# Transposing loads of a mixture-of-experts loop's rows, three sums buffers and six blocks per turn

## The chip, the cores and the metric

One core of a Trainium2 chip runs the whole kernel. The time is device microseconds (us) of one execution; the lower the better.

## The reference

Two samples of 1024 tokens with 256 channels pass a block with adaptive layer norm: linear attention with 8 heads of 32, then a mixture of 32 experts. All is float32. Cut to the part that the change touches:

```python
x = x + ga * attention(layernorm(x) * (1 + ca) + sa)
h = layernorm(x) * (1 + cb) + sb                 # (2048, 256)
scores = sigmoid(h @ w_router)                   # (2048, 32)
# per token: 4 of 8 groups by their two best, then the 6 best experts in them
combine[t, e] = scores[t, e] for the 6 chosen, else 0
g = einsum('th,ehm->etm', h, gate_w)             # m = 176
u = einsum('th,ehm->etm', h, up_w)
eo = einsum('etm,emh->eth', silu(g) * u, down_w)
routed = einsum('te,eth->th', combine, eo)
shared = silu(h @ sh_gate_w) * (h @ sh_up_w) @ sh_down_w
out = x + gb * (routed + shared)
```

## The kernel before

All five engines run programs written out by hand; semaphores order them, and PSUM banks are assigned by a plan (lines 215 to 320). Attention and the router work on tiles of 128 tokens in groups of four (GT); a sample b has two groups g. The names and lines that matter here:

- *Rows.* XH (line 85) holds per token 256 channels (X), 32 scores, and a record. `second_norm` on VectorE (L934) writes the normalised tokens h into X itself; TensorE turns them (`turn_h2`, L1311), ScalarE copies them out (`turned`, L686) and makes the scores (`scores`, L694; its activation is L698). `attend` (L871) holds, at its fourth tile, a reciprocal (L886) that waits for the store of the gate rows to DRAM (SP, L425).
- *Dispatch.* GpSimd writes each token's row to DRAM (`pair_rows`) six times, one indirect DMA per tile and choice, ordered by expert (L558).
- *The shared expert* (`hidden`, `shared_rows`) writes its rows to `token_sums[0]` (L711); the gated residual, divided by the gate, goes to `token_sums[1]` from SP (L431).
- *The loop over blocks.* A block is 128 (token, expert) pairs of one expert. A map in SBUF gives each block's expert and first row; the number of turns is known at run time only. `blocks` (L373) writes a step of R = 4 blocks five times on each engine: first, looped, twice under If, last. SP loads a block's rows (`load_rows`, L448) into one of four places once TensorE has turned what was there, and its records (`load_records`, L451). TensorE turns rows (`turn_x`, L1432) and, for blocks two apart, works through: turn the rows of n+2, turn the activations of n (`turn_act`, L1448), down of n-1 (`down_rows`, L1455), gate and up of n+2 (`gate_and_up`, L1440). VectorE copies the turned rows from PSUM (`copy_x`, L1105), multiplies (L1111), picks weights and token numbers (L1117, L1123). ScalarE does silu (L755), copies the turned activations (L762) and weighs the result (L769). GpSimd adds it into one of two sums in DRAM with an accumulating indirect DMA (`scatter`, L584); even blocks take `token_sums[0]`, odd ones `token_sums[1]`, and a scatter waits for the landing of the one two before it, which wrote the same sums. Blocks beyond the last non-empty one in a turn are run too, with destinations out of bounds.
- *The last stage.* SP fetches both sums in 8 groups of two tiles (L476; two groups of the first sums ahead of the last scatters), VectorE adds and multiplies by the gate (L1155, L1156), SP stores (L494).

## Time and profile before

| | |
|---|---|
| median of 3 runs | 584.3 us (577.68, 584.3, 585.07) |
| the profiled execution | 584.41 us, span 582.6 us |
| TensorE (PE) busy | 472.4 us, 81% |
| GpSimd (POOL) busy | 284.2 us, 49% |
| VectorE (DVE) busy | 232.7 us, 40% |
| ScalarE (ACT) busy | 176.3 us, 30% |
| matmuls of gate and up, L1444 | 416, 142.7 us busy |
| transposes of the rows, L1437 | 208, 40.7 us busy |
| DMA | 83.25 MB, mean 143 GB/s |

Times are from the start of the span. PEld is TensorE's weight load, SPq SyncE's DMA issue. Busy times of matmuls overlap, since matmuls are pipelined; the distance of their starts is what they cost. A float32 matmul appears twice, a transpose once. The idle time of an engine stands in brackets with what released it. The granted clock is TensorE's, as a share of full speed.

### The profile page before, as it was taken

The page shows a single profiled execution, that of the slowest core. Times are in us where ns is not written, and L with a number is a line of the kernel's source. Part 1 is how long each engine was busy: PE and PEld are TensorE (multiplying, and loading weights), DVE is VectorE, ACT ScalarE, POOL GpSimd, SP SyncE. Part 2 cuts the span into 40 slices and gives each one's busy share as a digit, 9 for nine tenths or more (in the row PEclk, how much of TensorE's full clock was granted, in tenths as well). Part 3 has the DMA queues.
Part 4 walks back from the last instruction along what each step waited for, and adds up shares of the span by engine and source line. Part 5 has one row for each costly group of instructions (what it writes and reads, how often), then busy time and mean ns, then how long its engine had stood idle before and what let it go on. Part 6 is the DMA issues. An engine that isn't in the chain of part 4 may idle for free.

```text
span 582.6 us, 9494 instructions
## 1 busy us (share of the span) xinstructions
PE 472.4 (81%) x1994; PEld 325.4 (56%) x1995; DVE 232.7 (40%) x983; ACT 176.3 (30%) x429; POOL 284.2 (49%) x253
## 2 busy tenths in 40 slices
PE   4898989827785459829699999999999999999800
PEld 3455755417534216415477777777777777777600
DVE  2726789405871027301133334334333333333206
ACT  2231322201220003001144444444444444444300
POOL 2303512770777731760045655665666666655630
PEclk9799978967895759958899999999999999999865
DMA  8999010330458842841257766567665757677459
GB/s 282 342 333 380 31 73 24 124 124 11 152 143 270 282 162 83 292 168 61 67 89 108 111 96 109 101 108 105 113 105 103 109 94 114 105 117 110 52 131 334
DMA packets 87922, 83.25 MB, mean 143 GB/s; under 512 B 22522, under 2 KB 80348, under 8 KB 87901
## 3 DMA queue, kind: packets, MB, share of 16 engines
q1 hardware_dynamic: 66012, 52.59, 31.1%
q0 software_dynamic: 19584, 28.33, 26.2%
q10 hardware_dynamic: 2304, 2.10, 1.1%
q8 instruction: 8, 0.13, 0.1%
q14 instruction: 14, 0.11, 0.1%
HBM read 43.13 MB, written 40.90 MB: 144 GB/s over the span
## 4 chain that ended last, share of the span: by engine, by line
PE 72%; issue 10%; DVE 7%; another core or an unknown queue 4%; DMA 4%; ACT 2%; SPq 1%; POOL 0%; POOLq 0%; ACTq 0%; DVEq 0%
PE bank L1444 21%; PE bank L1459 16%; PE bank L1361 8%; PE bank L1372 5%; PE bank L1437 4%; PE bank L1452 4%; PE bank L1261 4%; PE bank L1247 2%; PE bank L1334 2%; PE bank L1163 2%; DMA token_sums<-tok_buf,dest 1%; DMA XH<-in_L_attn_x 1%; PE bank L1280 1%; PE bank L1195 1%
## 5 line engine op out<-in xcount | busy, mean ns | idle before, releaser
L592 POOL DMA_INDIRECT token_sums<-tok_buf,dest x104 | 161.9, 1557 | 138.2 <-ACT tok_buf L775 52.2
L1444 PE MATMUL bank<-gate_up,tok_buf 128*128 x416 | 142.7, 466 | 0.4 <-DVE tok_buf L1109 0.4
L564 POOL DMA_INDIRECT pair_rows<-XH,rows_i x96 | 94.6, 985 | 62.7 <-DVE rows_i L1028 34.3
L1109 DVE COPY tok_buf<-bank 128x256 f32<-128x256 f32 x104 | 44.2, 425 | 172.2 <-PE bank L1437 143.8
L1459 PE MATMUL bank<-down,tok_buf 88*128 x416 | 109.9, 387 | 0.0
L1444 PEld LDWEIGHTS bank<-gate_up,tok_buf 128*128 128x128 f32 x416 | 80.0, 193 | 29.4 <-issue 2.1
L1459 PEld LDWEIGHTS bank<-down,tok_buf 88*128 88x128 f32 x416 | 71.0, 191 | 7.7 <-issue 0.2
L775 ACT ACTIVATE tok_buf<-bank,tok_buf 128x256 f32<-128x256 f32 x104 | 49.2, 473 | 55.0 <-PE bank L1459 28.7
L1361 PE MATMUL bank<-tok_buf,sh_gu 128*128 128x512 f32 (+1 forms) x96 | 50.1, 673 | 10.8 <-issue 10.8
L760 ACT ACTIVATE tok_buf<-bank 128x176 f32<-128x176 f32 x104 | 33.0, 317 | 79.9 <-PE bank L1444 73.3
L1437 PEld LDWEIGHTS bank<-ident,tok_buf 128*128 128x128 f32 x208 | 27.3, 141 | 37.9 <-issue 29.7
L1437 PE MATMUL bank<-ident,tok_buf 128*128 128x128 f32 x208 | 40.7, 277 | 6.6 <-issue 5.9
L766 ACT ACTIVATE tok_buf<-bank 88x256 f32<-88x256 f32 x104 | 39.4, 379 | 18.0 <-PE bank L1452 8.1
L1372 PE MATMUL bank<-sh_dn,sT 128*128 128x256 f32 (+1 forms) x96 | 27.9, 447 | 17.5 <-issue 17.5
L1361 PEld LDWEIGHTS bank<-tok_buf,sh_gu 128*128 128x128 f32 (+1 forms) x96 | 19.9, 209 | 39.6 <-issue 39.4
L1452 PE MATMUL bank<-ident,tok_buf 128*88 128x128 f32 x208 | 39.7, 273 | 0.0
L1115 DVE TENSOR_TENSOR tok_buf<-tok_buf,bank 128x176 f32<-128x176 f32 x104 | 34.1, 327 | 3.5 <-ACT tok_buf L760 3.5
L1372 PEld LDWEIGHTS bank<-sh_dn,sT 128*128 128x128 f32 (+1 forms) x96 | 21.1, 225 | 22.9 <-issue 19.2
L1261 PE MATMUL bank<-down 128*128 128x512 f32 x64 | 33.0, 652 | 0.0
L515 POOL TENSOR_SCALAR rstd<-gate_up 128x4 f32<-128x4 f32 x8 | 4.6, 571 | 43.9 <-DVE gate_up L932 30.3
L1119 DVE SCALAR_TENSOR_TENSOR tok_buf<-iota_e,own_expert,tok_buf 128x32 f32<-128x32 f32 x104 | 25.7, 247 | 0.4
L551 POOL TENSOR_TENSOR XH<-XH,down 128x256 f32<-128x256 f32 x16 | 11.0, 719 | 29.3 <-DVE down L869 29.3
(153 smaller groups left out, 462.6 us busy)
## 6 DMA issues: line engine op xcount, KB each, us to landing
tok_buf<-pair_rows SPq DMA_DIRECT2D x104, 128.0 KB
gate_up<-in_L_ffn_gate_w SPq DMA_DIRECT2D x8, 704.0 KB, 8.5
gate_up<-in_L_ffn_up_w SPq DMA_DIRECT2D x8, 704.0 KB, 9.1
down<-in_L_ffn_down_w SPq DMA_DIRECT2D x2, 2816.0 KB
pair_rows<-sh_rows SPq DMA_DIRECT2D x1, 5120.0 KB, 18.9
gate_up<-token_sums SPq DMA_DIRECT2D x16, 256.0 KB, 6.0
XH<-in_L_attn_x SPq DMA_DIRECT2D x4, 512.0 KB, 9.7
token_sums<-sh_rows ACTq DMA_DIRECT2D x16, 128.0 KB
```

The source lines that it names most:

```text
L564: nc.gpsimd.indirect_dma_start(out=pair_rows, out_offset=bass.IndirectOffsetOnAxis(ap=rows_i[:, t, k:k + 1], axis=0), in_=XH[:, t, :], in_ ...
L592: nc.gpsimd.indirect_dma_start(out=token_sums[c % 2], out_offset=bass.IndirectOffsetOnAxis(ap=dest[:, c:c + 1], axis=0), in_=yw[:, c, :], ...
L766: nc.scalar.activation(aT[0:KD, c % 2, :, :], banks[3][0:KD, 0:2 * P].rearrange("p (m n) -> p m n", m=2), ACT.Copy).then_inc(aT_copied, 1)
L775: nc.scalar.activation(yw[:, c, :], banks[4 + c % 2][:, 0:C], ACT.Copy, scale=pair_weight[:, c:c + 1]).then_inc(y_scaled, 1)
L1109: V.tensor_copy(xT[:, c % 2], banks[0][:, 0:C].rearrange("p (k n) -> p k n", k=KC)).then_inc(xT_copied, 1)
L1261: last = mm(ps[:, :], hT[:, k, a:a + P], wT[:, k, C:3 * C], start=k == 0, stop=k == KC - 1)
L1361: last = mm(ps[0:n, :], sh_gu[:, s, k, a:a + n], h2T[:, b, k, g * W:(g + 1) * W], start=k == 0, stop=k == KC - 1)
L1372: last = mm(ps[:, 0:C], sT[0:n, m, i * P:(i + 1) * P], sh_dn[0:n, m, :], start=m == 0, stop=m == len(SC) - 1)
L1437: last = nc.tensor.transpose(banks[0][:, k * P:(k + 1) * P], xg[:, s, k * P:(k + 1) * P], ident[:, :])
L1444: last = mm(banks[1 + c % 2][:, 0:M2], xT[:, c % 2, k, :], gate_up[:, bass.ds(e * (KC * M2) + k * M2, M2)], start=k == 0, stop=k == KC - 1)
L1452: last = nc.tensor.transpose(banks[3][0:KD, m * P:(m + 1) * P], act[:, c % 2, m * KD:(m + 1) * KD], ident[:, :])
L1459: last = mm(banks[4 + c % 2][:, 0:C], aT[0:KD, c % 2, m, :], down[0:KD, bass.ds(e * C + m * E * C, C)], start=m == 0, stop=m == 1)
```

## The change

- Rows go to DRAM as two planes of 16-bit halves: `second_norm` writes h to a buffer of its own (`h2`, one group), from which TensorE turns it, and ScalarE (`split`) writes the low halves of a token's 256 floats and then the high halves into X. VectorE waits with the next group's h for the split and the turned tiles of the last; GpSimd's dispatch waits for the split.
- In the loop SP loads a block's rows with a transposing DMA of 16-bit elements (128 rows x 512), and VectorE (`join_x`) interleaves low and high halves into float32. TensorE's `turn_x` and its PSUM bank are gone.
- R is 6: six places for rows, records, results; six blocks in a step; at least 17 turns where there were at least 24. The rings lie in XH's space.
- Three sums in place of two. A block adds into sums n mod 3, a scatter waits for the one three before it. `token_sums[2]` is filled with zeros by a DMA of SP behind that which clears the heads of `pair_rows`, ahead of the store of the gate rows.
- The last stage has 4 groups of four tiles. Each sums buffer is fetched whole once its last scatters have landed, the gate rows ahead of the third; VectorE adds the first two for all groups, then adds the third and multiplies.

The diff without its context lines (`@@ -n @@` is the line of the kernel before at which a part stands):

```diff
@@ -13 @@
-    f32, i32, u32, bf16 = mybir.dt.float32, mybir.dt.int32, mybir.dt.uint32, mybir.dt.bfloat16
+    f32, i32, u32, bf16, u16 = mybir.dt.float32, mybir.dt.int32, mybir.dt.uint32, mybir.dt.bfloat16, mybir.dt.uint16
@@ -37 @@
-    TURNS = -(-NBLK // 4)
-    FEWEST = T * TOPK // P // 4 - 1
-    MAP_W = P + 8
+    R = 6
+    NSUM = 3
+    TURNS = -(-NBLK // R)
+    FEWEST = T * TOPK // P // R - 1
+    MAP_W = P + 2 * R
@@ -73 @@
-        token_sums = [nc.dram_tensor(f"token_sums{a}", (T, C), f32).ap() for a in range(2)]
+        token_sums = [nc.dram_tensor(f"token_sums{a}", (T, C), f32).ap() for a in range(NSUM)]
@@ -94 @@
-        own_expert = sb("own_expert", [P, P])[:, :]
-        dest = sb("dest", [P, 4], i32)
+        own_experts = sb("own_expert", [P, P + R])
+        own_expert = own_experts[:, 0:P]
+        dest = sb("dest", [P, R], i32)
@@ -146 @@
+        h2 = part(GT * C).rearrange("p (i c) -> p i c", i=GT)
@@ -158 @@
-        part = shared_part(tok_buf, NT * C // 2)
-        R = 4
-        xg = part(R * C).rearrange("p (s c) -> p s c", s=R)
+        part = shared_part(XH[:, :, :].rearrange("p i w -> p (i w)"), NT * XW)
+        x_halves = part(R * C).bitcast(u16).rearrange("p (s q n) -> p s q n", s=R, q=2 * KC)
-        part = shared_part(tok_buf[:, NT * C // 2:], NT * C // 2)
@@ -175 @@
-        sums = gate_up[:, 0:2 * NT * C].rearrange("p (a i c) -> p a i c", a=2, i=NT)
+        sums = [*(gate_up[:, a * NT * C:(a + 1) * NT * C].rearrange("p (i c) -> p i c", i=NT) for a in range(2)), xn]
@@ -192 @@
-        var2_ready, rstd2_ready, h2_ready = (sem(n) for n in ("var2_ready", "rstd2_ready", "h2_ready"))
+        var2_ready, rstd2_ready, h2_ready, split_ready = (
+            sem(n) for n in ("var2_ready", "rstd2_ready", "h2_ready", "halves_ready"))
-        zeros_ready, heads_clear = sem("zeros_ready"), sem("segment_heads_clear")
+        zeros_ready, heads_clear, sums_clear = sem("zeros_ready"), sem("segment_heads_clear"), sem("last_sums_clear")
@@ -205 @@
-        x_turned, xT_copied, gu_done, silu_done, act_done, act_turned, aT_copied, y_done, y_scaled = (
-            sem(n) for n in ("x_turned", "xT_copied", "gate_up_done", "silu_done", "act_done", "act_turned", "aT_copied", "y_done", "y_scaled"))
-        OT = 2
-        fetched = [sem(f"sums_fetched{g}") for g in range(NT // OT)]
+        xT_joined, gu_done, silu_done, act_done, act_turned, aT_copied, y_done, y_scaled = (
+            sem(n) for n in ("xT_joined", "gate_up_done", "silu_done", "act_done", "act_turned", "aT_copied", "y_done", "y_scaled"))
+        OT = 4
+        fetched, last_fetched = ([sem(f"{n}_sums_fetched{g}") for g in range(NT // OT)] for n in ("first", "last"))
@@ -421 @@
+            sp.dma_start(token_sums[2].rearrange("(p n) c -> p n c", p=P),
+                         zeros[:, 0:C].unsqueeze(1).broadcast_to([P, NT, C])).then_inc(sums_clear, 16)
@@ -446 @@
-                sp.dma_start(xg[:, c, :], pair_rows[bass.DynSlice(col, P, E), 0:C]).then_inc(x_loaded[c], 16)
+                sp.dma_start_transpose(x_halves[:, c], pair_rows[bass.DynSlice(col, P, E), 0:C].bitcast(u16)).then_inc(x_loaded[c], 16)
@@ -462 @@
-                        sp.wait_ge(x_turned, n + 1)
+                        sp.wait_ge(xT_joined, n + 1)
@@ -475 @@
-                sp.dma_start(sums[:, a, t:t + OT, :], sums_v[a][:, t // TB, t % TB:t % TB + OT, :]).then_inc(fetched[g], 16)
-            early = 2
-            for a in range(2):
-                for s in range(a, R, 2):
+                sp.dma_start(sums[a][:, t:t + OT, :], sums_v[a][:, t // TB, t % TB:t % TB + OT, :]).then_inc(
+                    (fetched if a < NSUM - 1 else last_fetched)[g], 16)
+            for a in range(NSUM):
+                for s in range(a, R, NSUM):
-                for g in range(early):
-                    fetch_sums(a, g)
-                if a == 0:
+                if a == NSUM - 1:
-            for g in range(early, NT // OT):
-                for a in range(2):
+                for g in range(NT // OT):
-                sp.dma_start(out_v[:, t // TB, t % TB:t % TB + OT, :], sums[:, 0, t:t + OT, :]).then_inc(stored, 16)
+                sp.dma_start(out_v[:, t // TB, t % TB:t % TB + OT, :], sums[0][:, t:t + OT, :]).then_inc(stored, 16)
@@ -561 @@
+                    pool.wait_ge(split_ready, (t // GT + 1) * GT)
-                        out=pair_rows, out_offset=bass.IndirectOffsetOnAxis(ap=rows_i[:, t, k:k + 1], axis=0),
-                        in_=XH[:, t, :], in_offset=None).then_inc(dispatched, 16)
+                        out=pair_rows.bitcast(i32), out_offset=bass.IndirectOffsetOnAxis(ap=rows_i[:, t, k:k + 1], axis=0),
+                        in_=XH[:, t, :].bitcast(i32), in_offset=None).then_inc(dispatched, 16)
@@ -576 @@
+            pool.wait_ge(sums_clear, 16)
@@ -587 @@
-                wait(pool, scattered[(c - 2) % R], 16 * turns)
+                wait(pool, scattered[(c - NSUM) % R], 16 * turns)
-                    out=token_sums[c % 2], out_offset=bass.IndirectOffsetOnAxis(ap=dest[:, c:c + 1], axis=0),
+                    out=token_sums[c % NSUM], out_offset=bass.IndirectOffsetOnAxis(ap=dest[:, c:c + 1], axis=0),
@@ -599 @@
-                        scatter((c - 1) % R, n - 1, turn + (c == R - 1))
+                        scatter((c - 1) % R, n - 1, turn + (c > NSUM))
@@ -698 @@
+            def split(b, g):
+                for i in range(GT):
+                    t = b * TB + g * GT + i
+                    act_e.wait_ge(h2_ready, t + 1)
+                    nc.scalar.activation(X[:, t, :].bitcast(u16).rearrange("p (h c) -> p h c", h=2),
+                                         h2[:, i, :].bitcast(u16).rearrange("p (c h) -> p h c", h=2),
+                                         ACT.Copy).then_inc(split_ready, 1)
@@ -716 @@
+                        act_e.wait_ge(sums_clear, 16)
@@ -729 @@
+            split(0, 0)
+            split(0, 1)
@@ -740 @@
+            split(1, 0)
+            split(1, 1)
@@ -771 @@
-                    act_e.wait_ge(pool_passed, n - 1)
+                    act_e.wait_ge(pool_passed, n - R + NSUM + 1)
@@ -940 @@
+                if b or g:
+                    dve.wait_ge(split_ready, b * TB + g * GT)
+                    for k in range(KC):
+                        await_computed(dve, ("h2T", b, 0, k) if g else ("h2T", b - 1, NG - 1, k))
-                    V.scalar_tensor_tensor(out=X[:, t, :], in0=X[:, t, :], scalar=rstd2[:, t:t + 1],
+                    V.scalar_tensor_tensor(out=h2[:, i % GT, :], in0=X[:, t, :], scalar=rstd2[:, t:t + 1],
@@ -1099 @@
+            link(V.memset(own_experts[:, P:P + R], -float(2 * T)))
-            def copy_x(c, n):
-                dve.wait_ge(x_turned, n + 1)
+            def join_x(s, c, n, turn):
+                dve.wait_ge(x_loaded[s], 16 * (turn + 1))
-                V.tensor_copy(xT[:, c % 2], banks[0][:, 0:C].rearrange("p (k n) -> p k n", k=KC)).then_inc(xT_copied, 1)
+                V.tensor_copy(xT[:, c % 2].bitcast(u16).rearrange("p k (n h) -> p h k n", h=2),
+                              x_halves[:, s].rearrange("p (h k) n -> p h k n", h=2)).then_inc(xT_joined, 1)
@@ -1116 @@
-                V.scalar_tensor_tensor(out=rec[:, c, 0:E], in0=iota_e[:, :], scalar=own_expert[:, bass.ds(n, 1)], in1=rec[:, c, 0:E],
+                V.scalar_tensor_tensor(out=rec[:, c, 0:E], in0=iota_e[:, :], scalar=own_experts[:, bass.ds(n, 1)], in1=rec[:, c, 0:E],
-                    dve.wait_ge(pool_passed, n - 1)
-                V.scalar_tensor_tensor(out=dest[:, c:c + 1], in0=own_expert[:, bass.ds(n, 1)], scalar=-1.0,
+                    dve.wait_ge(pool_passed, n - R + NSUM + 1)
+                V.scalar_tensor_tensor(out=dest[:, c:c + 1], in0=own_experts[:, bass.ds(n, 1)], scalar=-1.0,
-                copy_x(c, c)
+                join_x(c, c, c, 0)
@@ -1135 @@
-                        copy_x(c, n + 2)
+                        join_x((c + 2) % R, c, n + 2, turn + (c + 2) // R)
@@ -1147 @@
+            def group(a, g):
+                return sums[a][:, g * OT:(g + 1) * OT, :]
+            for g in range(NT // OT):
+                dve.wait_ge(fetched[g], 32)
+                last = V.tensor_tensor(group(0, g), group(0, g), group(1, g), ALU.add)
+            link(last)
-                rows_g = slice(g * OT, (g + 1) * OT)
-                total = sums[:, 0, rows_g, :]
-                dve.wait_ge(fetched[g], 32)
-                link(V.tensor_tensor(total, total, sums[:, 1, rows_g, :], ALU.add))
-                V.tensor_tensor(total, total, over(gb_again[:, g * OT // TB, :], [P, OT, C], 1), ALU.mult).then_inc(out_ready, 1)
+                dve.wait_ge(last_fetched[g], 16)
+                link(V.tensor_tensor(group(0, g), group(0, g), group(2, g), ALU.add))
+                V.tensor_tensor(group(0, g), group(0, g), over(gb_again[:, g * OT // TB, :], [P, OT, C], 1),
+                                ALU.mult).then_inc(out_ready, 1)
@@ -1316 @@
-                        last = turn(of(keys[k])[:, i * P:(i + 1) * P], X[:, b * TB + g * GT + i, k * P:(k + 1) * P])
+                        last = turn(of(keys[k])[:, i * P:(i + 1) * P], h2[:, i, k * P:(k + 1) * P])
@@ -1429 @@
-            def turn_x(s, n, turn):
-                pe.wait_ge(x_loaded[s], 16 * (turn + 1))
-                wait(pe, xT_copied, n)
-                for k in range(KC):
-                    last = nc.tensor.transpose(banks[0][:, k * P:(k + 1) * P], xg[:, s, k * P:(k + 1) * P], ident[:, :])
-                last.then_inc(x_turned, 1)
-                pe.wait_ge(xT_copied, n + 1)
+                pe.wait_ge(xT_joined, n + 1)
@@ -1463 @@
-                turn_x(c, c, 0)
-            for c in range(2):
@@ -1473 @@
-                    if not last or c + 2 < R:
-                        turn_x((c + 2) % R, n + 2, turn + (c + 2) // R)
```

## Rows read from the trace of the kernel before

**Rows 1.** Table by stretch: busy PE, PEld, DVE, ACT, POOL; clock, DMA share, GB/s.
```profile
180.00:216.00 36.00, 18.96 (x48) 11.85 (x48) 0.68 (x4) 1.41 (x3) 23.22 (x25) 0.59 0.74 244
...
300.00:350.00 50.00, 50.00 (x239) 37.18 (x237) 17.95 (x99) 23.01 (x59) 28.76 (x19) 1.00 0.68 105
...
500.00:540.00 40.00, 39.97 (x190) 29.89 (x189) 14.70 (x80) 18.40 (x47) 23.73 (x16) 1.00 0.69 111
```

**Rows 2.** Timeline of one block: start us, us, engine, line, operation, [idle before].
```profile
382.85 0.38 PE L1437 MATMUL bank<-ident,tok_buf 128*128 128x128 f32 x2
...
383.07 0.38 PE L1452 MATMUL bank<-ident,tok_buf 128*88 128x128 f32 x2
...
383.29 1.03 PE L1459 MATMUL bank<-down,tok_buf 88*128 x4
...
383.40 0.33 SPq L449 DMA_DIRECT2D tok_buf<-pair_rows  x1
...
384.15 1.35 PE L1444 MATMUL bank<-gate_up,tok_buf 128*128 x4
...
385.34 0.38 PE L1437 MATMUL bank<-ident,tok_buf 128*128 128x128 f32 x2
```

**Rows 3.** Chain of waits, the loop: start us, us, what.
```profile
330.80 1.19 PE bank L1444 x4
...
513.69 1.19 PE bank L1444 x4
```

**Rows 4.** Groups by line and shape, 300 to 540: busy, mean ns, idle before.
```profile
L592 POOL DMA_INDIRECT token_sums<-tok_buf,dest x94 | 146.3, 1556 | 96.3 <-DMA token_sums<-tok_buf,dest 41.8 <-DVE dest L1126 22.2 <-issue 16.5
...
L1109 DVE COPY tok_buf<-bank 128x256 f32<-128x256 f32 x94 | 39.9, 425 | 146.6 <-PE bank L1437 118.2 <-issue 22.2 <-PE bank L1444 6.2
```

**Rows 5.** Timeline of the end.
```profile
552.66 1.98 PE L1459 MATMUL bank<-down,tok_buf 88*128 x8
...
556.34 1.56 POOL L592 DMA_INDIRECT token_sums<-tok_buf,dest  x1 [0.80 <-DMA token_sums<-tok_buf,dest]
...
558.49 1.55 POOL L592 DMA_INDIRECT token_sums<-tok_buf,dest  x1 [0.59 <-issue]
...
563.19 7.38 SPq L478 DMA_DIRECT2D gate_up<-token_sums  x14
...
577.62 0.69 DVE L1156 TENSOR_TENSOR gate_up<-gate_up 128x512 f32<-128x512 f32 x1
```

**Rows 6.** Chain of waits, the end.
```profile
551.71 3.80 DMA token_sums<-tok_buf,dest
...
558.49 4.64 DMA token_sums<-tok_buf,dest
```

**Rows 7.** Table by stretch, the end.
```profile
558.00:560.00 2.00, 0.00 (x0) 0.00 (x0) 0.00 (x0) 0.00 (x0) 1.51 (x1) 0.70 0.04 1
...
568.00:570.00 2.00, 0.00 (x0) 0.00 (x0) 1.96 (x4) 0.00 (x0) 0.00 (x0) 0.50 1.04 352
```

**Rows 8.** DMA queues, 300 to 540: packets, MB, share of 16 engines.
```profile
q0 software_dynamic: 13414, 11.49, 41.1%
...
q1 hardware_dynamic: 27072, 13.92, 25.1%
```

**Rows 9.** Table by stretch, the first stage.
```profile
52.00:56.00 4.00, 2.17 (x14) 1.56 (x13) 2.65 (x12) 0.66 (x2) 2.75 (x5) 1.00 1.05 382
...
56.00:60.00 4.00, 3.49 (x19) 3.30 (x19) 2.29 (x9) 0.77 (x2) 4.00 (x7) 0.63 0.88 317
```

**Rows 10.** Timeline of VectorE and ScalarE ahead of the loop.
```profile
63.37 3.32 DVE L886 RECIPROCAL down<-down 128x512 f32<-128x512 f32 x1
...
87.17 0.38 ACT L654 ACTIVATE down<-bank 128x256 f32<-128x256 f32 x1 [3.30 <-PE bank L1261]
...
160.92 0.60 ACT L709 ACTIVATE sT<-bank 128x512 f32<-128x512 f32 x1 [2.00 <-PE bank L1361]
...
216.41 0.38 ACT L720 ACTIVATE sh_rows<-bank 128x256 f32<-128x256 f32 x1 [1.19 <-remote]
```

## The prediction

> **What bounds the kernel now.** Three views decide, in this order. The table by stretch [rows 1] shows TensorE busy all of the 50 us from 300 to 350, at a granted clock of 1.00 (the level of 2.4 GHz), and 39.97 of the 40 us from 500 to 540: the loop over blocks of pairs, almost half of the span, runs at TensorE's pace. Beside it GpSimd has 28.76 us of the same 50, ScalarE 23.01, VectorE 17.95, and the 16 DMA engines a share of 0.68. From 180 to 216 it is neither: TensorE has 18.96 of 36 us at a granted clock of 0.59.
>
> The timeline of one block [rows 2] gives the order on TensorE; matmuls are pipelined, so starts count, not ends. Two transposes of the rows start at 382.85, those of the activations at 383.07, down at 383.29, gate and up at 384.15, the next rows at 385.34. So the rows' transposes take 0.22 us, the activations' 0.22, down 0.86, gate and up 1.19: 2.49 us a block. The chain of waits holds it over a distance: gate and up of one place in the turn start at 330.80 and at 513.69 [rows 3], 18 turns apart, 10.16 us a turn. That is 0.20 above 4 x 2.49: the boundary of a turn.
>
> **The change, part by part.** I sum against the profiled execution, 584.41 us with a span of 582.6; it is within 0.2 us of the median of the three runs, 584.3.
>
> *Rows that arrive turned.* TensorE loses 0.22 us a block and nothing else on it changes, so a block takes 2.27 us if no other engine is late. VectorE's copy of 256 floats from PSUM, 425 ns [rows 4], becomes a copy of 512 halves with a step of two. The trace has no such copy; the bounds are 0.425, if a half counts half, and 0.69, what 512 elements with two operands take [rows 5]. I take 0.65, near the upper one since the number of elements is the same. VectorE's busy time was 17.95 of 50 us, 0.91 a block; it becomes 1.14, at most 1.18, of 2.27: covered. The new copy waits for a load and for a product two blocks back, where the old one stood between a transpose and the product of its own block. ScalarE has 23.01 of 50, 1.17 a block. GpSimd's scatter is 1.556 us [rows 4]; with the 0.59 idle before the last one [rows 5] it is 2.15, covered as well, though narrowly.
>
> *Number of blocks.* Routing the reference's own inputs gives 102 non-empty blocks (each expert's tokens over 128, rounded up). Four per turn make 104 of them, six make exactly 102. The trace agrees that the last are empty: after the very last scatter starts, at 558.49 [rows 5], the DMA moves 1 GB/s until 560 [rows 7], against 105 in the loop. Two blocks go, 5.0 us. Boundaries fall from 25 to 16, but each loads half as many values again; 25 x 0.20 - 16 x 0.25 = 1.0.
>
> Loop: 102 x 0.22 = 22.4, and 5.0, and 1.0, and 0.4 for two row transposes ahead of the first block: **-28.8 us**. If something else holds the old pace, the blocks alone remain, -5.
>
> *The transposing load.* No row shows one. From below, it costs the DMA engines what the plain load does: from 300 to 540 queue q1 (rows and records) had 25.1% of 240 us, 60.2 us for 94 blocks, 0.64 a block, and q0 (scatters) 41.1%, 1.05 a block [rows 8]; together 1.69 of 2.27. From above: each 1 KB row is four pieces of 128 16-bit elements, and a piece costs what a mean packet costs now, 60.2 x 16 / 27072 = 35.6 ns; 512 + 128 packets then take 1.42 us, with the scatter 2.47. Further still, the whole 0.64 four times is 2.56, with the scatter 3.6. I take about 1.0, nearer to the plain load, since a piece has a quarter of the bytes: 2.05 of 2.27, just covered. SP's issue is 0.33 us now [rows 2] with another for the records; there is room for 1.6 more a block. The latency is covered by the six places: one is filled again 6 x 2.27 = 13.6 us before its rows are wanted. Behind a load on SP that waits for its join stand only record loads, which VectorE wants some blocks later.
>
> The Trainium skill stands on both sides here. "DMA: Bandwidth & Descriptors", section "Latency and other measured facts", has 261 GB/s for transposing DMAs over non-contiguous parts: an estimate from that page is 0.50 us for a block's 128 KB, and the loop would keep the sum above. "VectorE: DVE Perf Modes", section "The three transpose paths", has 1309 ns for one 128x128 16-bit transpose through the crossbar; four in a row would be 5.2 us a block by that page, twice the old pace. No row here shows either.
>
> *Three sums.* A scatter now waits for the one three before it. With two, waits for a landing were 41.8 us of GpSimd's idle time [rows 4]. Two blocks at the new pace are 4.54 us, and a landing came 3.80 and 4.64 us after its start [rows 6], so two sums would nearly bind; three give 6.8. No gain by itself: it is cover for the 22.4.
>
> *First stage.* A 2.1 MB zero fill goes on SP's queue ahead of the store of the gate rows. The DMA engines are full until about 59.5 us (382 GB/s, then a share of 0.88 from 56 to 60) [rows 9]; 2.1 MB at 382 is 5.5 us, so they are full until 65. What is late is VectorE's reciprocal at 63.37 [rows 10], which waits for that store, and all of attend behind it. 65 and a landing less 63.4: **+2.5**; 0 if the store overtakes, 5.5 at most.
>
> *The split on ScalarE.* 16 copies of 512 halves; a 128x512 activation is 0.60 us [rows 10], so 2.4 a group. Three groups find ScalarE idle behind the scores anyway: 3.30 us before 87.17, 2.71 likewise in the second group, 2.00 before 160.92 [rows 10], where the 0.4 left over delays nobody, as no bank is waited for. In the fourth it was idle for 1.19 before the shared rows at 216.41, for which TensorE waits: **+1.2**, between 0 and 2.4. The other new waits (split_ready on VectorE and GpSimd, the turned tiles) are for work that ended microseconds before.
>
> *The end.* TensorE's last matmuls run from 552.66 to 554.64, the last scatter starts at 558.49, and SP goes on at 563.19 [rows 5], 8.5 us after TensorE. With three sums the wait before 556.34 goes: 7. From there to 582.6 were 19.4 us. Now 6 MB are fetched where 4 were. Two sums, 4.2 MB, begin some 4.3 us before the last landing T; at 352 GB/s [rows 7] they take 12, until T + 8; gate rows and the first quarter of the third sum land at T + 11. VectorE then adds and multiplies four groups of 1024 elements, eight operations of 1.2 to 1.3 us (twice 0.69, less a start): T + 21. The last store, 512 KB, takes the 4.3 us that 256 KB took from the last product's end, 578.3, or a little more: T + 26. So -1.5 + 6.5 = **+5**; +1 if VectorE's work hides in the fetches, +9 if fetches and stores get in each other's way.
>
> Sum: -28.8 + 2.5 + 1.2 + 5 = -20.1; 584.4 - 20.1 = **564 us**.
>
> **The rivals.**
> *A. The DMA engines fill.* With 1.42 us for the loads a block takes 2.47 us: 102 x 0.20 = 20.4 given back, 585. For it: a share of 0.68 already. Against: a quarter of a row is not a whole packet's work. Chance 0.14.
> *B. Slower.* The queue turns rows one piece after the other at four times the present cost, and records behind them are held up too: 3.6 us a block, 102 x 1.33 = 136 more, 700. It decides from 2.27 + 20.1/102 = 2.47 us a block on. Nothing in the trace speaks against it but the plain loads' 0.64. The page with 1309 ns is on this side. Chance 0.14.
> *C. The blocks are not 102.* With 103 by the kernel's own routing there are 18 turns and 108 blocks, 6 x 2.27 = 13.6 more: 578. One token at a threshold would do it. Chance 0.04.
> *D. Longer stalls ahead of the loop.* From 180 to 216 ScalarE was busy for 1.41 us and TensorE half idle with the DMA engines at 0.74 [rows 1], and no wait for data accounts for it. More code on ScalarE and more DMA may lengthen that by a third, 12 us: 576. Chance 0.06.
>
> **How the numbers follow.** The forecast has 0.62, with a range of its own of 554 to 573: 0, 0 and +1 at one end (-27.8, and 2 for what the bounds miss), 5.5, 2.4 and 9 at the other (-11.9). A measurement of this kernel tells about 2%, 11.7 us: faster means below 572.6. Faster 0.62, the forecast. Slower 0.17: B and what of A lies beyond 596. Same 0.21: the rest. Range 552 to 590; it leaves out B and little else.
>
> **What would show it.** Right: gate and up 2.27 us apart at a clock of 1.00, a turn of 13.7 to 13.9; TensorE full; a DMA share of 0.85 to 0.95; VectorE's copy near 0.65; 102 scatters; 26 us from the last landing to the end; the reciprocal 2 to 3 us later. Wrong: TensorE idle in the loop and the copy waiting for the rows' DMA; issues on SP above 1.9 us; a DMA share of 1; 108 scatters; a copy above 1 us.

## The result, and the profile after

The changed kernel takes 596.3 us (median of 4 runs, 590.26 to 598.12) against 584.7 for the kernel before: ratio 1.023, 95% interval 1.018 to 1.029. It is slower by 2.3%; the forecast was 564. Its profiled execution has a span of 594.2 us, 11.6 more than before.

Three milestones split these 11.6 us, each read in the timeline of TensorE (the forecast had +2.5 + 1.2 - 0.4 ahead of the loop):

| | before | after | forecast |
|---|---|---|---|
| first gate and up product of the loop | 285.1 | 299.7: +14.6 | +3.3 |
| from there to the end of the last down product | 269.5 | 259.8: -9.7 | -28.4 |
| from there to the end | 28.0 | 34.7: +6.7 | +5 |

So of the 31.7 us between forecast and result, 18.7 lie in the loop, 11.3 ahead of it and 1.7 behind it.

**The loop.** The table by stretch (same columns as [rows 1]) shows TensorE no longer full, where it had 50.00 and 39.97:

```profile
300.00:350.00 50.00, 47.46 (x197) 33.41 (x197) 21.46 (x96) 20.48 (x58) 26.92 (x17) 0.96 0.71 95
500.00:540.00 40.00, 37.42 (x157) 27.09 (x158) 16.19 (x75) 16.86 (x47) 22.75 (x15) 0.96 0.78 107
```

The timeline of two neighbouring blocks answers [rows 2]. The rows' transposes are gone, and gate and up start 2.27 us apart:

```profile
372.83 1.35 PE L1465 MATMUL bank<-gate_up,XH 128*128 x4
...
375.10 1.35 PE L1465 MATMUL bank<-gate_up,XH 128*128 x4
```

So a block costs what was forecast. But over the 43 steps from 350.9 to 457.9 us the mean is 2.49, not 2.27: seven of them take 3.1 to 4.1 us. The chain of waits (start us, us, what) names who is late. In the loop of before it ran along TensorE [rows 3]; now the turn below lies wholly on SP's instruction queue, and over the whole execution 34% of the chain does (1% before):

```profile
404.75 2.67 SPq L369
...
413.72 1.19 SPq L453
...
415.16 0.37 SPq L456
...
415.74 1.19 SPq L453
...
417.13 0.42 SPq L456
...
417.76 1.19 SPq L453
...
419.98 2.73 SPq L369
```

A row load and a record load are issued every 2.02 to 2.04 us (415.74 to 417.76), and at each turn SP reads 12 values of the map from SBUF into registers (line 369) for 2.7 us. From 404.75 to 419.98 are 15.23 us for six blocks, 2.54 each: slower than TensorE's 2.27. In 330 to 500 us the trace has no wait of SP at all. The rows for single source lines (engine, operation, count, shortest/median/longest ns, first and last start) give the two prices. Of the kernel before:

```profile
L367 SPq TENSOR_LOAD <-down x27: 1666/1871/2041, 261.5 to 538.6; - x27
L367 PEldq TENSOR_LOAD <-down x27: 587/594/2335, 281.4 to 543.7; - x27
```

Of the changed kernel:

```profile
L453 SPq DMA_TRANSPOSE XH<-pair_rows x102: 668/1190/2215, 276.0 to 541.9; - x102
L369 SPq TENSOR_LOAD <-down x18: 2471/2660/3030, 273.2 to 546.1; - x18
L369 PEldq TENSOR_LOAD <-down x18: 846/2086/3405, 296.2 to 545.8; - x18
```

The issue of a transposing load holds SP's queue for a median of 1.19 us, where a plain one holds it for 0.33 [rows 2]. And on TensorE's own queue (PEldq) the read went from a median of 0.59 us to anything between 0.85 and 3.4. The median hides what it does; the same row for four consecutive turns:

```profile
L369 PEldq TENSOR_LOAD <-down x1: 3360/3360/3360, 314.7 to 314.7; - x1
L369 PEldq TENSOR_LOAD <-down x1: 1006/1006/1006, 330.2 to 330.2; - x1
L369 PEldq TENSOR_LOAD <-down x1: 3343/3343/3343, 343.8 to 343.8; - x1
L369 PEldq TENSOR_LOAD <-down x1: 1107/1107/1107, 359.2 to 359.2; - x1
```

Every second read takes some three times as long, from first to last. This turned out to be the heart of the case.

The other engines are as forecast: the copy of 512 halves takes 537 ns (0.65 had been taken), the scatter 1566, and the queue of rows and records, q1, 32.2% of 240 us, 77.3 us for 94 blocks: 0.82 a block, where "about 1.0" was taken. Groups from 300 to 540 us (columns as in [rows 4]), and the DMA queues (as [rows 8]):

```profile
L595 POOL DMA_INDIRECT token_sums<-XH,dest x92 | 144.0, 1566 | 124.9 <-ACT XH L792 64.4 <-issue 30.4 <-DMA token_sums<-XH,dest 19.2
...
L1131 DVE COPY XH<-XH 128x512 uint16<-128x512 uint16 x94 | 50.5, 537 | 3.6 <-issue 3.5
...
L1142 DVE SCALAR_TENSOR_TENSOR XH<-iota_e,own_expert,XH 128x32 f32<-128x32 f32 x94 | 23.6, 251 | 37.1 <-DMA XH<-pair_rows 33.5 <-issue 2.0
```

```profile
q0 software_dynamic: 13036, 11.16, 40.2%
q1 hardware_dynamic: 63185, 13.62, 32.2%
```

VectorE's 33.5 us of waiting (line 1142) is for the records, whose loads stand in SP's queue behind the slow issues.

**Ahead of the loop.** The timeline of the first stage: the zero fill's issue takes 11.3 us on SP's queue, and only behind it comes the store of the gate rows, for which the reciprocal waits (63.37 before, 66.47 now). Before, that store was issued at 50.90:

```profile
44.34 11.30 SPq L426 DMA_DIRECT2D token_sums<-sh_rows  x1
...
55.69 5.42 SPq L429 DMA_DIRECT2D gate_rows<-down  x1
```

```profile
66.47 3.35 DVE L903 RECIPROCAL down<-down 128x512 f32<-128x512 f32 x1 [4.41 <-DMA gate_rows<-down]
```

**The end.** The timeline (the counterpart of [rows 5]):

```profile
562.61 1.55 POOL L595 DMA_INDIRECT token_sums<-XH,dest  x1 [0.30 <-issue]
562.74 5.04 SPq L482 DMA_DIRECT2D gate_up<-token_sums  x8
572.63 0.32 SPq L489 DMA_DIRECT2D gate_up<-gate_rows  x1
572.99 1.94 SPq L482 DMA_DIRECT2D tok_buf<-token_sums  x4
...
581.49 1.23 DVE L1183 TENSOR_TENSOR gate_up<-gate_up,tok_buf 128x1024 f32<-128x1024 f32 x1 [0.83 <-DMA tok_buf<-token_sums]
```

and the chain beside it (as [rows 6]):

```profile
562.61 9.96 DMA token_sums<-XH,dest
...
572.99 8.38 DMA tok_buf<-token_sums
```

The last scatter starts 3.1 us after the end of TensorE's last product, not 3.9, but its landing takes 9.96 us where it took 4.64; the fetches of the first two sums were issued beside it, from 562.74 on. No run took them away, so that they are the cause is argued, not shown. Then come the third sum's fetch, 8.4 us, and eight operations of VectorE: 21.6 us from the landing to the end, where 26 were forecast.

### The profile page after: what moved, and what is told of

Read it like the earlier page. It is cut to its first block, busy times and chain, and to the rows that moved or that the text cites. A ratio compares the mean times of both kernels' runs of the same rounds, so it can differ in the third digit from the quotient of the medians.

```text
span 594.2 us, 8670 instructions
## 1 busy us (share of the span) xinstructions
PE 451.5 (76%) x1766; PEld 301.6 (51%) x1767; DVE 249.7 (42%) x970; ACT 173.9 (29%) x439; POOL 281.4 (47%) x251
## 4 chain that ended last, share of the span: by engine, by line
SPq 34%; PE 28%; issue 12%; another core or an unknown queue 10%; DMA 7%; DVE 5%; ACT 3%; POOLq 0%; DVEq 0%; ACTq 0%; POOL 0%
SPq L453 14%; PE bank L1390 7%; PE bank L1465 6%; SPq L369 5%; SPq L456 5%; SPq L419 4%; PE bank L1480 3%; PE bank L1401 3%; DMA token_sums<-XH,dest 2%; PE bank L1363 2%; SPq L426 2%; DMA gate_rows<-down 2%; DMA tok_buf<-token_sums 1%; PE bank L1192 1%
## 5 line engine op out<-in xcount | busy, mean ns | idle before, releaser
L595 POOL DMA_INDIRECT token_sums<-XH,dest x102 | 159.9, 1568 | 132.6 <-ACT XH L792 66.9
L1465 PE MATMUL bank<-gate_up,XH 128*128 x408 | 141.8, 470 | 9.1 <-issue 5.3
L1480 PE MATMUL bank<-down,XH 88*128 x408 | 106.0, 382 | 0.0
L1465 PEld LDWEIGHTS bank<-gate_up,XH 128*128 128x128 f32 x408 | 78.0, 194 | 41.0 <-issue 15.0
L1138 DVE TENSOR_TENSOR XH<-XH,bank 128x176 f32<-128x176 f32 x102 | 34.2, 336 | 113.3 <-ACT XH L777 96.6
L1480 PEld LDWEIGHTS bank<-down,XH 88*128 88x128 f32 x408 | 69.4, 190 | 6.6 <-issue 0.5
L792 ACT ACTIVATE XH<-bank,XH 128x256 f32<-128x256 f32 x102 | 48.3, 473 | 53.1 <-PE bank L1480 28.8
L1131 DVE COPY XH<-XH 128x512 uint16<-128x512 uint16 x102 | 54.3, 533 | 5.9 <-issue 5.8
L1473 PE MATMUL bank<-ident,XH 128*88 128x128 f32 x204 | 39.2, 274 | 14.9 <-DVE XH L1138 7.9
L1473 PEld LDWEIGHTS bank<-ident,XH 128*88 128x88 f32 x204 | 24.5, 124 | 46.1 <-issue 25.3
L783 ACT ACTIVATE XH<-bank 88x256 f32<-88x256 f32 x102 | 38.7, 379 | 15.8 <-PE bank L1473 14.4
L1390 PEld LDWEIGHTS bank<-tok_buf,sh_gu 128*128 128x128 f32 (+1 forms) x96 | 20.1, 211 | 32.8 <-issue 32.5
```

The lines of the kernel that those rows point to most:

```text
L595: nc.gpsimd.indirect_dma_start(out=token_sums[c % NSUM], out_offset=bass.IndirectOffsetOnAxis(ap=dest[:, c:c + 1], axis=0), in_=yw[:, c, : ...
L783: nc.scalar.activation(aT[0:KD, c % 2, :, :], banks[3][0:KD, 0:2 * P].rearrange("p (m n) -> p m n", m=2), ACT.Copy).then_inc(aT_copied, 1)
L792: nc.scalar.activation(yw[:, c, :], banks[4 + c % 2][:, 0:C], ACT.Copy, scale=pair_weight[:, c:c + 1]).then_inc(y_scaled, 1)
L1131: V.tensor_copy(xT[:, c % 2].bitcast(u16).rearrange("p k (n h) -> p h k n", h=2), x_halves[:, s].rearrange("p (h k) n -> p h k n", h=2)).t ...
L1390: last = mm(ps[0:n, :], sh_gu[:, s, k, a:a + n], h2T[:, b, k, g * W:(g + 1) * W], start=k == 0, stop=k == KC - 1)
L1465: last = mm(banks[1 + c % 2][:, 0:M2], xT[:, c % 2, k, :], gate_up[:, bass.ds(e * (KC * M2) + k * M2, M2)], start=k == 0, stop=k == KC - 1)
```

## Experiments

The loop times below run from the first gate and up product to the end of the last down product; 269.5 and 259.8 are those of the kernels before and after. Ratios are against runs of the kernel before on the same chip.

**1. Plain loads in place of transposing ones.** The rows arrive unturned, so the products are of the wrong data; the bytes, waits and places are the same.

```
-sp.dma_start_transpose(x_halves[:, c], pair_rows[...].bitcast(u16))
+sp.dma_start(x_halves[:, c]..., pair_rows[...].bitcast(i32))
```

> The kernel after with a plain load of the same 1 KB rows into the same places in place of the transposing one; the join then interleaves rows that are not turned, so the result is not the reference's. Theory S (SP's sequencer sets the pace: 1.19 us to issue a transpose, 0.84 with what lies around the record load, 2.7 for the register loads of a turn, 15.3 us a turn of six): SP needs about 0.35 + 0.84 a block and 2.7 a turn, some 10 us, so TensorE sets the pace, gate and up 2.27 us apart, a turn 13.7 to 13.9, the loop about 24 us shorter than after (235 against 260), the whole near 570. Theory E (the 16 DMA engines are too full with a share of 0.73 to serve pieces of 256 bytes): the same gain, with a DMA share of 0.75 or more of the shorter block. Theory V (VectorE's interleaving copy is late): no gain, 2.5 us a block.

570.7 us (a single execution), span 568.9. The loop took 249.2 us, 10.6 less, and SP had its 0.33 us issues. So the transposing load does cost the loop some 10 us. But between 350 and 450 us one step in twelve was still 3.8 to 4.1 us, all others 2.26 or 2.27: SP was not all of it. Another 14.0 us of the shorter span lie ahead of the loop (first product at 285.7, 299.7 in the changed kernel), where the two kernels have the same instructions. Keep this in mind for what follows: the first product of one profiled execution tells little.

**2. Half of the pieces.** Each load turns only the second 512 bytes of a row; the first half of the data is left out.

> The kernel after with only the upper halves of the rows loaded by the transposing DMA (128 rows x 256 columns of 16 bits, half the pieces); the lower halves are what lay there, so the result is not the reference's. Theory S with an issue that is the same for every transpose: 1.19 us again, a turn 15.3 us again, the whole within 1% of after (594). Theory S with an issue that grows with the number of pieces: about 0.7 us an issue, a turn 13.7, the whole near 575. Theory E: the issue stays at 1.19 but a turn falls below 14.5, since the engines have half of the pieces, and the DMA share falls with it.

588.0 us (a single execution), loop 257.9. Queue q1 fell to 17.3% of the DMA engines' time (31.7% in the changed kernel, 330 to 500 us in both), while the issue did not move:

```profile
L453 SPq DMA_TRANSPOSE XH<-pair_rows x102: 765/1169/1818, 270.7 to 535.1; - x102
```

What binds is the instruction on SP's queue, not the transfer on the DMA engines; and half the tiles do not shorten it.

**3. The records' loads on ScalarE's queue.** SP then reads six values a turn.

```
-load_records((c + 1) % R, cols[c + 1])          # on SP
+act_e.wait_ge(dest_ready, n + 3 - R)            # on ScalarE
+load_records((c + 2) % R, cols[c])
```

> The kernel after with the record loads issued by ScalarE, and six register loads a turn on SP and on ScalarE in place of twelve on SP. Theory S: SP needs 6 x 1.6 + 1.4 + 0.4 = 11.4 us a turn, so TensorE sets the pace with 13.6 to 13.9, and the loop loses 9 to 10 us for 102 blocks at the least and 24 at the most: 570 to 585 for the whole, ratio to the kernel before 0.975 to 1.00. ScalarE gains 0.4 a block and 1.4 a turn over 1.17 a block, 11 us of 13.7. Theory E: the bytes and pieces are the same, so a turn stays at 15.3 and the ratio at 1.02.

584.2 us, ratio 1.002 (0.997 to 1.006), loop 252.0. The waits of SP's queue from 330 to 500 us came back:

```profile
SPq L453 <- DVE XH L1136: 37.0, 23, 2.6
```

SP was no longer the bound, and still one step of 3.9 to 4.3 us remained in each dozen, that is in every second turn (the even turns' reads of about 1.1 us cost 0.1 to 0.4).

**4. The zero fill behind the gate rows' store.**

> The kernel after with the zero fill of the third sums put behind the store of the gate rows on SP's queue. The loop starts 14.7 us later after than before (299.7 against 285.0). Theory F (the fill ahead of the store makes the reciprocal and all of attend late, and the later stages only carry that on): the reciprocal starts at 63.4 again, the router scores of the first group at 84 where they were at 89.2, and the loop starts 5 to 6 us earlier, near 294, the whole near 589. Rival G (the stalls of the instruction streams between 98 and 300 move with the DMA traffic and take up any gain): the first scores are 5 us earlier but the loop starts less than 2 us earlier. What is left over either (9 us) is then due to the split and to stalls.

584.2 us, ratio 1.003 (0.999 to 1.008). The reciprocal starts at 63.82, the first scores at 83.89 (89.19 in the changed kernel, 83.60 before) and the first gate and up product at 290.0; the loop is as it was, 260.7. The store of the gate rows is issued at 51.26, and the fill behind it takes SP's queue 1.56 us. So of the 5.6 us by which the scores were late the order of the two gives back 5.3, and the whole gains 2.0% by the two ratios (1.003 and 1.023). All runs bear out the scores: with the fill first (the changed kernel, 1, 2, 3, 9) they start at 87.9 to 89.2, in all others at 80.9 to 83.9.

**5. Both together (3 and 4).**

> The two earlier edits together: the zero fill issued behind the gate row's store, and the records' loads issued by ScalarE's queue. Theory (SP's queue is the loop's bound, the fill ahead of the gate row the first stage's): the gains add. First gate and up product at about 288 us (290.0 with the late fill, 292.6 with the records moved, 299.7 with neither), loop from there to the last down product about 252 us (252.0 with the records moved), tail 34: span 574, time about 576, ratio 0.985. Rival (what lies ahead of the loop is stalls that fall anew in each kernel, not the fill): first product at 293 to 299 and 580 to 586 us.

582.2 us, ratio 0.987 (0.979 to 0.995); on this chip the kernel before took 588.8, so the time is the rival's and the ratio the theory's (0.985). The loop is as expected, 252.8. The first product of the profiled execution is at 296.3, where the rival had it, not 288, but by the ratios the late fill gains 1.5% here too (1.002 in experiment 3). The two signs disagree. The ratios rest on several executions each, the first product on one, and experiment 1 shows how far that one moves; so I go by the ratios.

**6. As 5, TensorE's queue reads 9 values, not 12.**

```
-experts = load_values(pe, PE, 0, turn, -1)          # 2 * R values
+experts = load_values(pe, PE, 0, turn, -1, R + 3)
```

> As e5_late_and_act, but TensorE's queue reads 9 values of the map at each turn (the ones it uses) and not 12. Theory (a turn's boundary costs TensorE 1.5 to 1.9 us because its queue reads the 12 values one after another, median 2.26 us a turn with the records moved): the read takes 1.7 us or less, each of 18 boundaries is 0.5 us shorter, loop 243 us, time 9 us below e5_late_and_act. Rival (the boundary waits for another thing, a branch or a code fetch, or VectorE's copy): the same time as e5_late_and_act within 2 us.

569.2 us, ratio 0.967 (0.959 to 0.976). The loop took 244.7, 8.1 less than in 5: the read was the boundary's cost. Another 8.9 us of the profiled execution lie ahead of the loop (first product at 287.5), where the two kernels have the same work, as in experiment 1. The reads on odd turns fell from between 3.3 and 3.6 us to between 2.3 and 2.9, some 0.28 us for each value less; on even turns they stayed at 0.85 to 1.2. That left a question: what do odd turns have?

**7. The unrolling alone.** The kernel before with R = 6, its rings in the rows' array, two sums.

> The kernel before with the unrolling alone: six blocks a turn with its rings in the rows' array, two sums buffers, rows loaded plain and transposed on TensorE, last stage as before. 102 blocks in place of 104 save 5 us. Theory (12 values read on TensorE's queue take 2.1 us at a boundary in place of 0.6 for 8): 17 boundaries of 1.7 us more, less 26 of 0.3 us that go, add about 20 us: loop 280 to 285 us in place of 269.5, time 595 to 600. Rival (the read is hidden while TensorE still works off its queue, and the boundary gap of the changed kernel comes from the transposing load): loop 263 us, time 578.

614.2 us, ratio 1.044 (1.035 to 1.053), loop 294.8: more than the theory said. The timeline of TensorE at one boundary of an odd turn, and the table of that stretch (columns as in [rows 1]):

```profile
404.25 1.35 PE L1445 MATMUL bank<-gate_up,XH 128*128 x4
407.86 0.60 PE L1438 MATMUL bank<-ident,XH 128*128 128x128 f32 x2 [2.25 <-issue]
...
410.39 1.86 PE L1445 MATMUL bank<-gate_up,XH 128*128 x4
```

```profile
408.00:412.00 4.00, 4.00 (x12) 3.01 (x12) 0.91 (x5) 0.85 (x2) 0.53 (x1) 0.57 0.54 70
```

The read (2.98 us) leaves TensorE idle for 2.25 us, and then its granted clock is 0.57 for the next 4 us, near the level of 1.2 GHz, and the next block takes its transposes, down, gate and up at about half the pace. The step is 6.14 us in place of 2.49: the stall costs 3.65, not 2.25.

**8. Two sums in the changed kernel.** No zero fill, no third fetch.

> The changed kernel with two sums buffers in place of three: no zero fill, no third set fetched and added at the end, a scatter waits again for the one two blocks before. Theory (the third buffer costs the fill ahead of the loop and about 6.5 us at the end, and gives the loop nothing): first stage as with the late fill, first gate and up product at 290, loop 258 to 260, tail 28 to 29, time about 578. Rival (with SP's queue late and rows landing late, scatters two blocks apart hold the loop): loop 266 or more, time 586 or more.

599.6 us, ratio 1.019 (1.011 to 1.027); loop 263.7, and 38.5 from its end. The time is the rival's; the loop lies between theory (258 to 260) and rival (266 or more), nearer to the rival. From 380 us on, but for a stretch from 532 to 550, the chain ran mostly from landing to landing of scatters:

```profile
498.80 4.13 DMA token_sums<-XH,dest
503.86 4.92 DMA token_sums<-XH,dest
509.60 4.67 DMA token_sums<-XH,dest
515.20 4.30 DMA token_sums<-XH,dest
```

Two blocks per 5.1 to 5.7 us is 2.5 to 2.9 a block. So at a pace of 2.27 two buffers would bind, and the third is needed. This is worked out from the landings; two sums with the mended reads of experiment 9 were not run.

**9. The same values, read from aligned places.** TensorE's read of turn t starts at word 6t of the map, byte 24t counted from the map's start: a multiple of 16 on even turns, 8 bytes off on odd ones. In the kernel before it started at byte 16t. SP's start is never a multiple of 16: 4 bytes past one in the kernel before, 4 or 12 past one in the changed kernel. So the map was copied once into 12 words a turn, which costs VectorE four small copies:

```
+for a in range(2):
+    for h in range(2):
+        V.tensor_copy(by_turn[a, t, h*R:(h+1)*R], map_i[a][(t+h)*R + a ...])   # all t at once
-map_i[0:1, bass.ds(section * MAP_W + 1 + first + R * turn, 2 * R)]
+by_turn[0:1, bass.ds(section * 2 * TURNS * R + 1 - section + first + 2 * R * turn, count)]
```

> The changed kernel with the map's values for each turn copied once (four copies of 132 values by VectorE) into a table of 12 words a turn, so that every read on TensorE's and SP's queues starts at a multiple of 16 bytes. So far TensorE's read of 12 values took 0.85 to 1.1 us on even turns (start at a multiple of 48 bytes) and 3.0 to 3.7 us on odd ones (24 bytes further), and SP's, which starts 4 bytes off, 2.7 us on each. Theory (the start decides): every read takes 0.8 to 1.2 us, TensorE's loop goes to about 2.30 us a block and SP's turn to 13.6 us; from the first gate and up product to the last down product 240 us in place of 259.8, time 576. Rival (the odd turns are slow for another cause, such as code or the queue's state): the reads keep 3.0 us or more on odd turns, time 596.

568.1 us, ratio 0.970 (0.964 to 0.976): 3.0% faster than the kernel before, and by the two ratios (0.970/1.023) 5.2% faster than the changed one. The loop took 235.3, the four copies together 1.14 (from 259.03). On TensorE's queue every read but the very first takes 0.86 to 1.26 us; the first still starts 4 bytes off and takes 3276 ns. Here are the reads, and the table from 330 to 500 us (TensorE's busy time is its second number), first of this kernel:

```profile
L372 SPq TENSOR_LOAD <-down x18: 710/754/1022, 268.1 to 516.9; - x18
L372 PEldq TENSOR_LOAD <-down x18: 855/1103/3276, 293.6 to 518.6; - x18
```

```profile
330.00:500.00 170.00, 170.00 (x751) 125.00 (x750) 84.20 (x375) 81.26 (x225) 117.87 (x76) 1.00 0.85 119
```

then of the changed kernel:

```profile
330.00:500.00 170.00, 155.64 (x671) 110.46 (x669) 72.89 (x340) 73.02 (x202) 106.45 (x68) 1.00 0.73 106
```

All 44 steps that start between 350 and 450 us are 2.26 or 2.27. SP's turn fits too: 15.23 less 1.9 (2.66 less 0.75) is 13.3, under 6 x 2.27 = 13.6, and its issues are as dear as ever.

**10. As 9, with the zero fill late.**

> As e9_by_turn_table with the zero fill behind the gate row's store. Theory: what each gives adds, first gate and up product at 288 to 291, loop 240, tail 34.5, span 564, time 566, ratio 0.965. Rival (SP's queue keeps the loop, its transposes' issue of 1.19 us being the bound and the reads not): loop 252 or more, time 580.

563.6 us, ratio 0.962 (0.955 to 0.970), the fastest of all, though its interval overlaps that of 9. Loop 236.0, first product at 290.8 (297.1 in 9). The span of its profiled execution, 561.0, is 21.6 us under that of the kernel before; the forecast was 20.1. So with these two mends, which move a table and swap two transfers, the change gives in the whole what it was forecast to give, though not part by part: the loop wins more, and what lies ahead of it and behind it costs more.

**11. As 7, with the table.**

> e7_six_alone (the kernel before, six blocks a turn, nothing else) with the same table. Theory (the 6.1 us steps on every second turn of e7_six_alone come from the slow read and the clock it costs, 0.57 granted in 408 to 412 us there): steps of 2.5 to 2.9 us, loop about 258 to 262 us in place of 294.8, time 576 to 580. Rival (they come from the longer body of the loop): 605 or more.

587.2 us, ratio 1.007 (1.002 to 1.013). The steps of 6.1 us are gone (longest 3.26 between 350 and 450), loop 266.7: 28 us less than in 7, so the longer code was not the cause. The loop missed the theory by 5 us and the time by 7; why its boundaries still take up to 3.26 us is open. Unrolling by itself, well aligned, gave 2.8 us in the loop, and the whole is still 0.7% slower than the kernel before.

**12. The kernel before, its map two words further on.** The write of the map moves with the read; nothing else differs.

```
-map_i[0:1, bass.ds(section * MAP_W + 1 + first + R * turn, 2 * R)]
+map_i[0:1, bass.ds(section * MAP_W + 3 + first + R * turn, 2 * R)]
```

> The kernel before with nothing changed but the map's place: two words (8 bytes) further on, so that TensorE's reads of 8 values, which start at multiples of 16 bytes and take 0.59 us, start 8 bytes off. Theory: each takes 2.0 to 2.4 us, 26 boundaries of 1.2 to 1.7 us more, time 615 to 630 (more where the clock falls). Rival (the start does not matter): 584, ratio 1.00.

623.6 us, ratio 1.065 (1.059 to 1.070). TensorE's reads of the same 8 values, 0.594 us before:

```profile
L367 PEldq TENSOR_LOAD <-down x27: 1932/2093/2339, 285.6 to 583.6; - x27
```

Between 350 and 450 us each boundary takes 4.06 to 4.30 us where it took 2.61 to 3.12, and the loop takes 307.2 us (269.5 before). SP's read, off in both, stays at 1.88. A shift by 8 bytes makes the kernel 6.5% slower.

## Why the prediction was wrong

*The step that failed is the boundary of a turn*: "Boundaries fall from 25 to 16, but each loads half as many values again; 25 x 0.20 - 16 x 0.25 = 1.0". The read on TensorE's queue was scaled by the number of its values. Its real price hangs on where it starts: 0.07 to 0.09 us a value from a multiple of 16 bytes (0.594/8; 1.103/12), 0.25 to 0.28 from 8 bytes off (2.093/8; 2.97 to 3.41 over 12). Going from four to six blocks a turn moved every odd turn to the dear kind. Experiment 12 makes this cost in the kernel before by the shift alone, and 9 takes it out of the changed one and changes no transfer. The boundaries were forecast at 16 x 0.25 = 4.0 us in all; aligned reads, on both queues, made the loop 24.5 us shorter (259.8 to 235.3), more than the 18.7 by which it had missed. The trace of before held the warning: the first of its 27 reads, which starts one word further, took 2335 ns beside a median of 594, and SP's, with the same number of values, 1871.

*"SP's issue is 0.33 us now ... there is room for 1.6 more a block"* left out two things: a transposing load's issue, 1.19, and SP's read. Six times (1.19 + 0.37 + what lies between, 2.03 in all) is 12.2 us, and 2.7 for the read: with the rest of the turn 15.2, more than 13.6. The Trainium skill has a price for the second, though it tells there of the runtime's own register loads: "Runtime: NRT & Kernel Launch", section "Instruction fetch mechanics", has some 200 ns for each register that is loaded. The trace agrees roughly where the start is off (SP 1871/8 = 0.23), and not where it is a multiple of 16 bytes (0.07). An estimate from that page is 2.4 us for 12 values, 0.4 a block. With the 0.33 us issues of the forecast SP would still have seemed free; with the measured 2.03 a block it is past 2.27.

The two overlap, so they cannot be added: freeing SP alone (3) brought the loop from 259.8 to 252.0, the aligned reads, which help both queues, to 235.3. What TensorE's read costs by itself is shown in the kernel before alone (12, where SP's read is unchanged: 37.7 us of loop for 26 boundaries); in the changed kernel, with SP's left as it was, it was not run.

*The rest of the loop was right.* A block is 2.27 us, and there are 102. The copy takes 0.54 (forecast 0.65), a block's loads 0.82 of the DMA engines (about 1.0), the DMA share in experiment 9 is 0.85, and as far as 8 shows three sums are needed. With the reads mended the loop is 235.3, even 5.8 below the forecast's 241.1; 4.0 of these are the boundaries, which then cost nothing.

*Rivals.* A (the DMA engines fill) and B (a queue that turns rows at 3.6 us a block) did not come: experiment 2 halves the pieces and the loop gains 1.9 us, and in 9 whole rows arrive at one block per 2.27 us. The bound on SP's issue that "would show it wrong" was put at 1.9 us; 1.56 was enough, with the read beside it.

*Ahead of the loop*, +14.6 against +3.3. The forecast's +2.5 had the right wait, the reciprocal's for the store of the gate rows, but reckoned with busy DMA engines alone. In the trace the fill's issue holds SP's queue for 11.3 us, and the store is issued at 55.69 in place of 50.90. The reciprocal is 3.1 us late, and the scores 5.6. By the ratios a late fill gains 2.0% (4 against the changed kernel), 1.5% (5 against 3) and 0.8% (10 against 9, where the intervals overlap). The other 9 us of the +14.6 build up between 110 and 300 us. Rival D said that stalls which no wait for data accounts for would lengthen. There are such stalls in both traces, but on TensorE they sum to some 46 us of these 190 now and to some 56 before, and experiment 1, with the same instructions as the changed kernel there, starts its loop 14.0 us earlier. So whether the change causes these 9 us, or they fall anew in each kernel, stays open, and with it the split on ScalarE, which was not tried alone.

*The end*, +6.7 against +5: the mechanism was right, and two sizes were off that nearly cancel, which is luck. The last landing was taken as one of before (4.64), though it was known that 4.2 MB would be fetched beside it: 9.96. And from it to the end were 21.6 us, not 26.

## What to carry to other kernels

When an engine's queue reads register values from SBUF in the path of a loop, look at where the read starts as a function of the turn: changing the unroll factor changes the alignment, and a read that costs nothing at one factor binds at another; a table with a stride of a multiple of four words cost 1.1 us of copies and gave 5%. Price each instruction on the queue that issues it (a transposing load's issue, a register read), not only its bytes, and sum a whole turn of that queue against the engine that sets the pace. Look at the shortest and longest of an operation, not at its median: one outlier among 27 rows told the price here. And do not judge what lies ahead of a loop by one profiled execution when kernels with the same instructions there differ by 14 us; compare the times of several.

## What was unexpected of the hardware

- Reading 8 words from SBUF into registers on TensorE's queue takes 0.59 us from a start at a multiple of 16 bytes and 2.09 us from 8 bytes off; on SP's queue 12 words take 0.75 against 2.66.
- Issuing a transposing load of 128 rows of 1 KB takes SP's queue 1.19 us (median), and half of each row hardly less (1.17); a plain one 0.33.
- After TensorE had been idle for 2.25 us the block behind it ran at a granted clock of 0.57 (experiment 7), and after two more such gaps, at 442 and 476, slowly too. In the changed kernel gaps of 1.2 to 1.6 us did not do that, nor did one of 2.87 us before 469.17 (granted clock 1.00 from 330 to 500), so the length of the gap alone does not tell. The ends of matmuls are modelled, so these gaps are too.
- A scatter that adds landed in 9.96 us with 4.2 MB of fetches beside it, and in 4.64 without (one of each).
